# Layer 0's softmax denominators: spread over the partitions by two DMAs through DRAM in place of a TensorE matmul

## What is computed

```
qkv  = conv1x1(groupnorm(x), w_qkv) + b_qkv        # 576 channels
qkv  = depthwise_conv3x3(qkv, w_dw) + b_dw
q, k, v = split(qkv); each (2, 4 heads, 48, 4096)
q, k = q / norm(q), k / norm(k)                    # over the 48 channels of a head
attn = softmax(q^T k * temperature)                # 4096 x 4096 for each of 8 heads
out  = attn v;  x = x + conv1x1(out, w_proj) + b_proj
```

## Time and profile before

| | us |
|---|---|
| median of 3 runs | 3994.99 (3993.24 to 3997.37) |
| the profiled execution | 3993.2 |
| its span, first to last instruction | 3991.4 |
| TensorE matmuls busy in the span | 3574.1 (90%) |
| VectorE busy | 2171.5 (54%) |
| ScalarE busy | 2221.6 (56%) |
| GpSimd busy | 342.2 (9%) |
| mean granted TensorE clock | 0.957 of full |

### The profile page before, as it was taken

How to read it: one execution, slowest core, us unless ns; L and a number is a source line. 1 busy time by engine, 2 the same in 40 slices (tenths; PEclk the granted TensorE clock), 3 DMA queues, 4 the chain that set the end, 5 groups by cost and what they waited for, 6 DMA issues and landing times. The chain is left out here.

```text
span 3991.4 us, 53719 instructions
## 1 busy us (share of the span) xinstructions
PE 3574.1 (90%) x18516; PEld 1946.7 (49%) x18516; DVE 2171.5 (54%) x2749; ACT 2221.6 (56%) x2690; POOL 342.2 (9%) x124
## 2 busy tenths in 40 slices
PE   1269999999999999999997679999998669999999
PEld 0022322223222232222222358888886248888888
DVE  4744157331565234652014457777776447777777
ACT  0036555465555655556661257777773147777776
POOL 0212012020110201101001200000000300000000
PEclk9579999999999999999998889999999789999999
DMA  6221112121121211102003520101012350010100
GB/s 178 55 56 32 40 35 66 36 43 41 33 55 36 50 37 37 50 18 51 3 5 93 162 81 25 29 24 30 24 29 70 107 148 24 25 28 24 30 24 18
DMA packets 166881, 194.73 MB, mean 49 GB/s; under 512 B 28802, under 2 KB 105474, under 8 KB 164994
## 3 DMA queue, kind: packets, MB, share of 16 engines
q1 hardware_dynamic: 166724, 192.65, 18.8%
HBM read 106.01 MB, written 50.92 MB: 39 GB/s over the span
## 5 line engine op out<-in xcount | busy, mean ns | idle before, releaser
L413 ACT ACTIVATE prob<-ps_s,cur 128x1024 f32<-128x1024 f32 x1024 | 1085.5, 1111 | 794.4 <-PE ps_s L493 792.8
L506 PE MATMUL ps_a<-prob,vt 128*64 128x512 f32 x4096 | 997.6, 608 | 0.0
L1277 PE MATMUL ps_s<-kst,qs 128*128 128x512 f32 x2560 | 690.2, 401 | 47.6 <-DMA qs<-q_scratch 34.7
L1298 PE MATMUL ps_o<-v_hl,at_hi 128*128 128x384 f32 x2048 | 646.3, 372 | 2.3 <-DVE at_lo L1505 2.3
L487 PE MATMUL ps_s<-q_a,k_a 128*128 128x512 f16 x2048 | 537.6, 385 | 10.1 <-issue 5.1
L1298 PE MATMUL ps_o<-v_hl,at_lo 128*128 128x192 f32 x2048 | 513.1, 251 | 0.0
L1277 PEld LDWEIGHTS ps_s<-kst,qs 128*128 128x128 f32 x2560 | 448.3, 190 | 120.4 <-issue 37.2
L506 PEld LDWEIGHTS ps_a<-prob,vt 128*64 128x64 f32 x4096 | 249.6, 136 | 412.9 <-issue 412.2
L1505 DVE TENSOR_TENSOR at_lo<-ps_t,at_hi 128x512 fp32r<-128x512 f32 x512 | 351.6, 687 | 155.8 <-ACT at_hi L1143 146.9
L487 PEld LDWEIGHTS ps_s<-q_a,k_a 128*128 128x128 f16 x2048 | 142.9, 98 | 520.5 <-ACT prob L413 412.6
L1476 DVE TENSOR_REDUCE nmx<-ps_s 128x1 f32<-128x1024 f32 x256 | 311.5, 1217 | 153.9 <-PE ps_s L1277 153.9
(11 more groups left out here) (143 smaller groups left out, 2902.9 us busy)
## 6 DMA issues: line engine op xcount, KB each, us to landing
z<-z_scratch SPq DMA_DIRECT2D x96, 384.0 KB, 3.6
q_scratch<-qst SPq DMA_DIRECT2D x64, 384.0 KB, 5.0
qs<-q_scratch SPq DMA_DIRECT2D x64, 384.0 KB, 3.8
sq<-rn_scratch SPq DMA_DIRECT2D x16, 768.0 KB, 10.2
gn_x<-in_x SPq DMA_DIRECT2D x4, 1536.0 KB, 18.4
z_scratch<-gn_x SPq DMA_DIRECT2D x4, 1536.0 KB, 11.6
q_a<-hi SPq DMA_DIRECT2D x64, 96.0 KB, 2.3
o_scratch<-o_s SPq DMA_DIRECT2D x64, 96.0 KB, 1.9
```

The lines of the kernel that those rows point to most:

```text
L413: act.activation(prob[:, a % PR, :], ps_s[:, a % 2, :], ACT.Exp, bias=cur[:, slot:slot + 1], scale=1.0 / SPLIT).then_inc(exped, 1)
L506: ins = pe.matmul(ps_a[h * HALF:(h + 1) * HALF, j % 2, :], vt[:, slot, m, :], prob[:, a % PR, h * CH:(h + 1) * CH], start=(m == 0), stop=( ...
L1277: ins = pe.matmul(ps_s[:, c % 2, h * CH:(h + 1) * CH], qs[:, s, qt, :], kst[:, ktile, cols], start=(t == 0), stop=(t == len(terms) - 1))
L1298: ins = pe.matmul(ps_o[:, 0:wide], a[:, j % 4, m * P:(m + 1) * P], v_hl[:, kt, 0:wide], start=(kt == 0 and t == 0), stop=(kt == KT - 1 and ...
```

## The change

The selection matrix and its matmul go. In their place SP writes partitions 48 and 112 of `acc_s` (two rows of 512 values) to a DRAM scratch, waits for it, and reads each row back into 48 partitions of `rden`. VectorE waits for both and takes the reciprocal in place. The DMAs stand in SP's list just ahead of the store of the same block. The helper tile is used four times less in a head.

```
-USE_EVEN = 8 + 2 + 8 + 4
-USE_ODD = 8 + 2 + 8 + 8 + 4
+USE_EVEN = 8 + 2 + 8
+USE_ODD = 8 + 2 + 8 + 8
-DEN_AT = {1: 16, 2: 8, 3: 12}
...
 (SyncE)
-                sp.dma_start(den_sel[:, :], consts["den_sel"]).then_inc(const_in, 16)
...
+                def denominators(g, j):
+                    at = NBL * g + j
+                    sp.wait_ge(acc_free, at + 3)
+                    sp.dma_start(den_dram[bass.ds(g, 1), j * NB:(j + 1) * NB].rearrange("o (h n) -> (o h) n", h=2),
+                                 acc_s[HD::HALF, :]).then_inc(den_out, 16)
+                    sp.wait_ge(den_out, 16 * (at + 1))
+                    for h in range(2):
+                        sp.dma_start(rden[h * HALF:h * HALF + HD, :],
+                                     den_dram[bass.ds(g, 1), j * NB + h * CH:j * NB + (h + 1) * CH].partition_broadcast(HD)
+                                     ).then_inc(den_in, 16)
...
+                    denominators(g, 0)
                     store_block(g, 0)
-                    sums_out(base + 11, g + 1)
+                    sums_out(base + 10, g + 1)
                     norms_out(g + 1)
+                    denominators(g, 1)
                     store_block(g, 1)
                     split_out(1, g + 1, 2 * STEPS * g + 1)
+                    denominators(g, 2)
                     store_block(g, 2)
+                    denominators(g, 3)
                     store_block(g, 3)
...
 (GpSimd)
+                pool.memset(rden[:, :], 1.0)
...
 (TensorE)
-                def denominators(g, j, use):
-                    n, bank = use
-                    helper_free(n)
-                    pe.wait_ge(acc_free, NBL * g + j + 3)
-                    pe.matmul(ps_h[:, bank, :], den_sel[:, :], acc_s[:, :], start=True, stop=True).then_inc(help_full, 1)
...
                             prep(j, m, uses)
-                            if j >= 1 and m == DEN_AT[j]:
-                                denominators(g, j - 1, uses.next())
-                    denominators(g, NBL - 1, uses.next())
...
 (VectorE)
-                def finish(g, j, use):
-                    n, bank = use
-                    full(n)
-                    dve.reciprocal(rden[:, :], ps_h[:, bank, :]).then_inc(help_free, 1)
-                    dve.wait_ge(help_free, n + 1)
-                    dve.wait_ge(o_stored, NBL * g + j + 1)
+                def finish(g, j):
+                    at = NBL * g + j
+                    dve.wait_ge(acc_free, at + 3)
+                    dve.wait_ge(den_in, 32 * (at + 1))
+                    dve.reciprocal(rden[:, :], rden[:, :]).then_inc(den_over, 1)
+                    dve.wait_ge(den_over, at + 1)
+                    dve.wait_ge(o_stored, at + 1)
                     dve.tensor_tensor(o_s[:, j % 2, :], acc_s[:, :], rden[:, :], ALU.mult).then_inc(o_op, 1)
```

More of the change, by code:

```diff
@@ L154, in next, with layer0 @@
         return self.base + self.n - 1, (self.n - 1) % 2
-def layer0(nc, z_dram, w_qkv, vecs, temperature, consts, ss_dram, rn_dram, o_dram):
+def layer0(nc, z_dram, w_qkv, vecs, temperature, consts, ss_dram, rn_dram, den_dram, o_dram):
     with ExitStack() as ctx:
@@ L195, in layer0 @@
         ones_blk = sb("ones_blk", [P, P])
-        den_sel = sb("den_sel", [P, P])
         temp = sb("temp", [P, B * HEADS])
@@ L230, in layer0 @@
         acc_free = sem("acc_free")
+        den_out = sem("den_out")
+        den_in = sem("den_in")
+        den_over = sem("den_over")
         o_op = sem("o_op")
@@ L240, in layer0 @@
         STEPS = NBL * KT
-        NCONST = 4
+        NCONST = 3
         with nc.Block() as block:
@@ L351, in pair @@
                         load_z(range(4), 3 * i + 4, nxt, base + 5)
+                    denominators(g, 0)
                     store_block(g, 0)
                     if not last:
-                        sums_out(base + 11, g + 1)
-                        load_z(range(4, 8), 3 * i + 4, nxt, base + 12)
+                        sums_out(base + 10, g + 1)
+                        load_z(range(4, 8), 3 * i + 4, nxt, base + 11)
                         norms_out(g + 1)
+                    denominators(g, 1)
                     store_block(g, 1)
                     if not last:
-                        load_z(range(4), 3 * i + 5, nxt, base + 16)
+                        load_z(range(4), 3 * i + 5, nxt, base + 15)
                         split_out(0, g + 1, 2 * STEPS * g + 1)
+                    denominators(g, 2)
                     store_block(g, 2)
+                    denominators(g, 3)
                     store_block(g, 3)
@@ L515, in head @@
                         if a == 0:
-                            pe.wait_ge(help_free, base - 1)
+                            pe.wait_ge(help_free, base)
                         weigh(a)
@@ L733, in even @@
                     copy_acc(g, 0)
-                    finish(g, 0, uses.next())
+                    finish(g, 0)
                     for q in range(2):
@@ L739, in even @@
                     copy_acc(g, 1)
-                    finish(g, 1, uses.next())
+                    finish(g, 1)
                     split(g + 1)
                     copy_acc(g, 2)
-                    finish(g, 2, uses.next())
+                    finish(g, 2)
                     dve.wait_ge(pv_done, STEPS * g + 1)
@@ L747, in even @@
                     copy_acc(g, 3)
-                    finish(g, 3, uses.next())
+                    finish(g, 3)
                 def odd(i, last):
@@ L1576, in build @@
 def build(nc, a, out):
-    consts = {k: a[k] for k in ("group", "mean", "ident", "ones_blk", "den_sel")}
+    consts = {k: a[k] for k in ("group", "mean", "ident", "ones_blk")}
     z_dram = nc.dram_tensor("z_scratch", [B, C, N], F32, kind="Internal").ap()
@@ L1580, in build @@
     rn_dram = nc.dram_tensor("rn_scratch", [2, N], F32, kind="Internal").ap()
+    den_dram = nc.dram_tensor("den_scratch", [B * HEADS, N], F32, kind="Internal").ap()
     o_dram = nc.dram_tensor("o_scratch", [B * HEADS, HD, N], F32, kind="Internal").ap()
@@ L1586, in build @@
     group_norm_and_store(nc, a["x"], consts, z_dram)
-    layer0(nc, z_dram, a["w_qkv"], a["vecs"], a["temperature"], consts, ss_dram, rn_dram, o_dram)
+    layer0(nc, z_dram, a["w_qkv"], a["vecs"], a["temperature"], consts, ss_dram, rn_dram, den_dram, o_dram)
     o_by_image = o_dram.rearrange("(b h) d n -> b (h d) n", b=B)
@@ L1640 @@
         "ones_blk": ((block_of[:, None] == block_of[None, :]) & (block_of[:, None] >= 0)).astype(f),
-        "den_sel": (rows[:, None] == (rows[None, :] // HALF) * HALF + HD).astype(f),
     }
```

## The result

The changed kernel takes 3943.9 us (median of 4 runs, 3941.7 to 3945.4) against 3996.1 us before (4 runs); the ratio is 0.987, 95% interval 0.9853 to 0.9887. The forecast was 3955 us, faster, in a range of 3936 to 3975. The profiled execution took 3943.7 us with a span of 3941.7: 49.5 us less than before's profiled one, where the steps had given 40.

What follows compares the result with a forecast made beforehand. TensorE's work list was taken to bound layer 0 (busy 1845 of 1878 us). Terms 20.2 + 13.4 + 10.8 + 2.2 - 3.3 = 43.3 us, less 3 for clock drops, left 40: 3955 us, range 3936 to 3975.

Steps and rivals of the forecast that it cites:

- (a): Blocks 0, 1 and 2 where nothing is waited for: 21 matmul slots of 0.96 us leave TensorE, 20.2 us gained.
- (e): Ends of heads 0, 2, 4, 5, 6: pairs shorten from 5.77 to 3.61 us, 10.8 us gained.
- (b): The DRAM round trip replacing the matmul: 4.5 us from copy's end to VectorE's start, against 1.28; bounds 4.1 to 7.4.
- The price of a longer trip: Third rival, a 7.4 us trip: each us more paid twice in three odd heads, once at the end; 3975, chance 0.15.
- (c): Block 1: the denominators' write waits behind the two norms' broadcasts; in head 1 the reciprocal comes 1.5 us later.
- The rival that it overtakes: Block 1's small write passes the broadcasts, both waits of (d) go, no clock drop: 3935 us, chance 0.10.
- (d): Block 2 of heads 1, 3, 5: one 6.63 us wait becomes two, 3.0 and 2.6 us; 13.4 us gained.
- the 3 us: Deduction from the 43.3 us sum for new clock drops: one in three behind the second wait of (d), rounded up.
- The second rival: Clock falls at every new TensorE wait, both in each odd head, waits not swallowing it: 3965 us, chance 0.15.
- (f): Ends of heads 1 and 3, TensorE's jump back: begins 1.1 us earlier, same length, low clock kept; 2.2 us gained.
- (g): Last block of head 7: nothing covers the trip, 4.5 us against 1.28; 3.3 us lost.

Runs made afterwards that it cites:

- the reordered one: The changed kernel with block 1's trip put between the norms' write and the two broadcasts, not behind them: 3924.1 us, ratio 0.9822 to before.
- the kernel with the filled jump: The changed kernel with two unneeded matmuls behind the last transposes of heads 1, 3 and 5, ahead of TensorE's jump back: 3941.4 us, ratio 0.9867.

## Why the prediction was right, and which term was off

**(a), (e)** Right to 0.1 us. What made them easy is that TensorE's pairs are as regular as a clock: the difference of two pairs is the price.

**(b)** The trip alone was put at 4.5 us; it is 4.4 to 4.8 where nothing stands ahead of it, and 5.5 at the two jumps, where the two reads' issues take 1.7 us and not 0.86. But the step "alone in their queue in all places but one" is wrong: block 2 of the four even heads has the moves of the split parts ahead of it in SyncE's list, and the trip takes 20.1 to 21.1 us, where 4.1 to 5 was to show the step. The sum was spared because TensorE needs nothing from VectorE there so soon, the slack that (a) names; but 16 us more had not been held against it, and that it was enough is luck. The price of a longer trip, put at 7 for 1, came out as 8 when it was doubled.

**(c)** Right in kind. Recomputed from the copy's new time the reciprocal comes 0.7 us later than in the kernel before against its head, where 1.5 was forecast; the write was held 11.6 us. The rival that it overtakes is refuted, by the changed kernel's rows and by the reordered one, and its price was too low: it had 3935, the reorder gives 3924. For block 3 of the odd heads the rival had 30.5 us and 29.7 came; what it lacked stands at the jumps, 11.7 us from before to the reordered kernel, where the sum had 2.2.

**(d)** Right in mechanism: one wait became two, for the convolution and for the first copy of v. Waits of 3.0 and 2.6 us were forecast, 2.35 and 0.53 came, with 3.4 us of half clock between them, which takes up most of the second: head 3 of the kernel with the filled jump had no half clock and waits of 2.03 and 2.46 us. (The items added to 9.7 there sum to 9.6, which changes nothing.) Sized at 13.4 less a share of the 3 us, measured 15.5 with the clock in it. The second rival, a drop of the clock at every wait that adds to it, is wrong in that last part: the drop came in all three heads, but behind the first wait, where the second swallows it.

**(f)** This is the term that was mis-sized: 2.2 us against 8.0, some six of the nine and a half us by which the sum fell short. The step read "The jump stays as long, but can begin when the transposes are out". It begins much earlier. TensorE's sequencer runs ahead of its queue of matmuls; in the changed kernel its branch record starts at 706.1 us, as the last `weigh` matmuls begin, 2.1 us before the last transposes, and lasts 4.6 us. Before, the sequencer stood at the wait for the copy and the branch started at 721.46, with 3.45 us still to go. The next score came 5.36 us after the last transposes' start then (719.72 to 725.08) and comes 2.69 after it now. And I let the low clock stay as it was; now half clock was granted for 3.4 us, not 6.8 (the pair behind takes 4.81 us, not 5.98), and in six of the eight experiments not at all. How long a given jump takes, and whether the clock falls behind it, stays open: the branch records last 3.3 to 4.6 us for the same code.

**(g)** 3.3 forecast, 3.7 measured with all that follows (3.1 of it is VectorE's longer wait).

**The clock.** 3 us were taken off for new drops. They did come, in all three odd heads, but each took the place of a longer one (3.4 us of half clock for 6.8, 10.2 and 6.8). Without this deduction and with the jump right the sum would have been 49.1.

## What to carry to other kernels

Where one engine's list is the limit, compare the pair of work units with and without an instruction: that is its price. A wait just ahead of a loop's jump is paid again, since it keeps the sequencer from starting the jump. A DMA round trip of 4.5 us may replace a 1 us matmul if the engine that waits for it is not the limit; then look at what is ahead of it in the queue, since putting it ahead of two broadcasts was worth 14 of the 20 us that this version was faster, and use the matmul where nothing covers the trip.

## What the runs showed of the hardware

- A write of 4 KB to DRAM behind two broadcasts of 768 KB each took 11.6 to 12.4 us to its release, 1.7 alone.
- TensorE's jump back, 3.3 to 4.6 us in the branch records, is worked off under matmuls already queued; 1.9 us of added matmuls in it cost nothing.
- Half clock (1.2 GHz) was granted for 3.4 us after a single idle stretch of 2.35 us, and at the jumps after 2.08 and 1.98 us, but not after 1.96 us at a jump of another kernel, nor after 2.03 and 2.46 us in head 3 of the kernel with the filled jump. So the length of one idle stretch does not settle it here. After 6.63 us it lasted 6.8 to 10.2 us.
- The reciprocal of 128x512 f32 takes 3.353 us from SBUF and 3.358 from PSUM.
